# A layer with paged attention on one core: order of stores and gathers, values alone, and who scales and who adds

## The reference, cut to what matters

```python
x = x + einsum('bct,bcd->bdt', x, W0[cond])                  # mix of the 32 tokens, by a condition
x = x + x @ W.T + lora(x, A[adapter], Bm[adapter]) * s       # dense layer plus an adapter of rank 16
# attention: 8 query heads, 4 key heads, head size 32, window 128, blocks of 16 rows of a paged cache
q, k, v = x @ Wq.T, x @ Wk.T, x @ Wv.T;  q, k = rope(rms(q)), rope(rms(k))
k_blocks = k_blocks.at[blk, :, off, :].set(k)                # new rows are written into the cache first,
v_blocks = v_blocks.at[blk, :, off, :].set(v)                # and any sequence may read a block that another wrote
x = x + softmax(mask(q @ k_all.T * SCALE)) @ v_all @ Wo.T
x = x + x @ W3[expert] + b3[expert]                          # one of 16 experts for each sequence
```

## Time and profile before

| | us |
|---|---|
| median of three runs | 156.03 (155.38 to 156.3) |
| the profiled execution | 154.9 |
| its span in the trace | 153.1 |

### The profile page before, as it was taken

One profiled execution on the slowest core, in us unless ns is written; L12 is line 12 of the kernel. 1 busy time (PEld: TensorE's weight loads), 2 busy tenths in 40 slices (PEclk: granted clock), 3 DMA queues, 4 the chain that ended last, 5 costly groups with the idle time before them and its releaser, 6 DMA issues.

```text
span 153.1 us, 4138 instructions
## 1 busy us (share of the span) xinstructions
PE 117.3 (77%) x1418; PEld 91.0 (59%) x1418; DVE 88.8 (58%) x315; ACT 85.8 (56%) x236; POOL 62.0 (41%) x65
## 2 busy tenths in 40 slices
PE   7569599999989586076598392892599999999762
PEld 7559458998374163074466272672387787776631
DVE  0597988857528824860344003610867999989361
ACT  3119634698743629256589721472438878888200
POOL 7666779000008764787233300330333444734000
PEclk9999999999999977659969758699569999999999
DMA  3982999999963444799739998999976676766110
GB/s 94 244 249 62 370 424 407 423 405 374 395 173 100 132 119 114 247 313 392 315 110 269 422 355 210 401 377 279 253 232 205 197 242 204 222 207 180 37 39 34
DMA packets 29100, 37.60 MB, mean 246 GB/s; under 512 B 9497, under 2 KB 26781, under 8 KB 27438
## 3 DMA queue, kind: packets, MB, share of 16 engines
q1 hardware_dynamic: 26136, 23.98, 50.0%
q0 software_dynamic: 2528, 12.82, 22.2%
q10 hardware_dynamic: 416, 0.56, 1.2%
HBM read 31.39 MB, written 10.04 MB: 271 GB/s over the span
## 4 chain that ended last, share of the span: by engine, by line
DMA 42%; PE 20%; SPq 17%; issue 9%; POOL 5%; DVE 3%; ACT 2%; POOLq 1%; DVEq 0%
DMA kv_rows<-blkp 15%; DMA wr_rows<-blkp 11%; PE bank L1117 5%; DMA blkp<-wr_rows,patch_i 4%; PE bank L1063 4%; POOL wr_rows L500 4%; DMA blkp<-in_L_cond_W 4%; PE bank L1075 3%; PE bank L1128 3%; SPq L386 3%; DMA mask_rows<-span_m 3%; DMA scal<-in_L_cond_scalings 3%; SPq L364 2%; SPq L365 2%; SPq L348 2%
## 5 line engine op out<-in xcount | busy, mean ns | idle before, releaser
L520 POOL TENSOR_TENSOR xin_m<-xin_m,ri 128x704 f32<-128x704 f32 x15 | 21.8, 1454 | 44.4 <-DVE ri L924 44.4
L674 ACT ACTIVATE xin_m<-kvn_m,nb 128x176 f32<-128x176 f32 x64 | 27.6, 443 | 9.2 <-DVE nb L911 9.2
L911 DVE CUSTOM_DVE_ANT_0 kvn_m<-bank,mask_m 128x176 f32<-128x176 f32 x64 | 18.0, 336 | 14.6 <-PE bank L1063 11.0
L951 DVE TENSOR_TENSOR blkp<-blkp,cst 128x512 f32<-128x512 f32 x16 | 15.6, 1015 | 17.6 <-DMA blkp<-in_L_cond_W 17.6
L1063 PE MATMUL bank<-kt_m,natQ 32*64 32x176 f32 x256 | 15.7, 366 | 10.0 <-DVE nb L911 9.1
L1063 PEld LDWEIGHTS bank<-kt_m,natQ 32*64 32x64 f32 x256 | 9.5, 150 | 14.2 <-issue 13.1
L500 POOL DMA_INDIRECT wr_rows<-kvn_m,row_i x8 | 8.8, 1104 | 21.3 <-DMA wr_rows<-blkp 19.1
L684 ACT COPY x_m<-bank 128x512 f32<-128x512 f32 x16 | 9.4, 590 | 13.0 <-PE bank L1075 12.8
L1043 PE MATMUL bank<-cst,blkp 121*128 121x121 f32 (+1 forms) x48 | 9.0, 352 | 7.8 <-DMA blkp<-wr_rows,patch_i 7.8
L1043 PEld LDWEIGHTS bank<-cst,blkp 121*128 121x128 f32 (+1 forms) x48 | 7.3, 190 | 10.0 <-DMA blkp<-wr_rows,patch_i 9.0
L674 ACT ACTIVATION_READ_ACCUMULATOR xin_m<-kvn_m,nb 128x1 f32 x64 | 12.8, 200 | 0.0
(11 more groups left out here) (194 smaller groups left out, 257.4 us busy)
## 6 DMA issues: line engine op xcount, KB each, us to landing
blkp<-in_L_cond_W SPq DMA_DIRECT2D x32, 256.0 KB, 3.5
kv_rows<-blkp SPq DMA_DIRECT2D x3, 2048.0 KB, 10.3
wr_rows<-blkp SPq DMA_DIRECT2D x1, 1536.0 KB, 16.5
mask_m<-mask_rows SPq DMA_DIRECT2D x32, 44.0 KB, 5.4
vm_m<-kv_rows SPq DMA_DIRECT2D x4, 320.0 KB, 4.4
xin_m<-in_x SPq DMA_DIRECT2D x2, 512.0 KB, 5.6
out<-wq_m SPq DMA_DIRECT2D x8, 128.0 KB, 3.5
vm_m<-kv_rows SPq DMA_DIRECT2D x2, 384.0 KB, 4.6
```

The costliest lines, as they stand in the source:

```text
L520: pool.tensor_tensor(e_, e_, ri[:, p % 2, :].unsqueeze(2).broadcast_to([P, 4, KEYS]), ALU.mult).then_inc(s_pn, 1)
L674: act.activation(pr_seq(n % 2, u, j), S[:, n % 2, u, j, :], ACT.Exp, bias=nb[:, n % 2, 2 * u + j:2 * u + j + 1], scale=-1.0, accum_out=rs[ ...
L911: dve.tensor_tensor_reduce(S[:, n % 2, u, j, :], bank[2 + (2 * n + u) % 3][:, j * KEYS:(j + 1) * KEYS], mask[:, 2 * n + j, :], -SCALE, 3e3 ...
L951: tt(w_, w_, ident.unsqueeze(1).broadcast_to([P, B4, P]), ALU.add).then_inc(s_wx, 1)
```

## The change

- The store of the written blocks goes ahead of all masks, in SyncE's list; the masks come in smaller lots: 16 behind it, 4 behind `values_out(0)`, 4 behind `values_out(1)`, 8 behind `values_out(2)`. Each lot of 8 has its own semaphore, and VectorE waits for a lot at every fourth pair.
- GpSimd issues the gathers of units 1 and 2 only when both halves of NU are permuted. Their four permutes are all done by VectorE, behind the rotations; before, ScalarE did three of them.
- `values_out` stores the values alone (512 B pieces, 121 or 110 partitions) to `v_rows`, instead of keys and values of 128 partitions.
- Patches 0 and 1 are issued together, patch 2 behind the landing of `values_out(0)`.
- `values_out(u + 1)` stands behind four experts, no longer ahead of them. Experts 8 to 15 go to `blkp[1]`, not `blkp[2]`.
- Key chunks 4 and 5 are turned within the loop (two in each of the first four steps), and q tiles 4 to 7 in steps 3, 4, 6, 7. VectorE does the last six pieces of q's norm and rotation within the loop, one a step in steps 0 to 5.
- In the loop VectorE scales the probabilities of every pair, and GpSimd adds the identity to the expert weights and then gathers that group's bias.

```diff
-            for b in range(8):
-                load_mask(b)
             for kv in range(2):
                 sp.wait_ge(s_perm[NU, kv], 1)
             sp.dma_start(wr_blocks, blkw[0:NWI, :]).then_inc(s_base, 16)
-            for b in range(8, B):
+            for b in range(2 * MB):
                 load_mask(b)
...
-                        u = (0, 2)[b // 8]
+                        u = b // 8
                         sp.wait_ge(s_kt, 4 * (u + 1))
                         sp.wait_ge(s_vo[u], 16)
...
-                sp.dma_start(kv_rows[u], blkp[u][:, :]).then_inc(s_vo[u], 16)
+                sp.dma_start(v_rows[u, 0:PU[u]], by_o[u][0:PU[u], :, 1, :]).then_inc(s_vo[u], 16)
...
             values_out(0)
+            for b in range(2 * MB, 2 * MB + 4):
+                load_mask(b)
             values_back(0)
-            values_out(1)
             for b in range(4):
                 expert(b)
+            values_out(1)
+            for b in range(2 * MB + 4, 3 * MB):
+                load_mask(b)
             values_back(1)
-            values_out(2)
             for b in range(4, 8):
                 expert(b)
+            values_out(2)
+            for b in range(3 * MB, B):
+                load_mask(b)
             values_back(2)
...
-            for i in ((NU, 0), (NU, 1), (0, 0), (0, 1), (1, 0), (1, 1)):
+            for i in ((NU, 0), (NU, 1), (0, 0), (0, 1)):
                 load_blocks(i)
...
+            for kv in range(2):
+                pool.wait_ge(s_perm[NU, kv], 1)
+            load_blocks((1, 0))
+            load_blocks((1, 1))
             pool.wait_ge(s_l0, 4)
             load_blocks((2, 0))
             pool.wait_ge(s_vz, 1)
             load_blocks((2, 1))
...
-            for u in range(NU):
+            def patch(u):
...
+            patch(0)
+            patch(1)
+            pool.wait_ge(s_vo[0], 16)
+            patch(2)
             pool.wait_ge(s_eidi, 1)
             pool.wait_ge(s_l1, 4)
-            for n in range(NT):
-                pool.indirect_dma_start(out=be[n], ...)
-            for p in range(PAIRS - 1):
-                pool.wait_ge(s_ri, p + 1)
-                pool.tensor_tensor(e_, e_, ri..., ALU.mult).then_inc(s_pn, 1)
+            for g in range(NT):
+                pool.wait_ge(s_we[g % B4], 16 * B4 * (g // B4 + 1))
+                for kc in range(KC):
+                    w_ = We4(g)[:, :, kc, kc * P:(kc + 1) * P]
+                    ptt(w_, w_, ident.unsqueeze(1).broadcast_to([P, B4, P]), ALU.add).then_inc(s_wx, 1)
+                pool.indirect_dma_start(out=be[g], ...)
...
-            permute((2, 0))
+            for i in ((1, 0), (1, 1), (2, 0), (2, 1)):
+                permute(i)
...
                     dve.reciprocal(ri[:, p % 2, :], rs[:, p % 2, :]).then_inc(s_ri, 1)
+                    dve.wait_ge(s_ri, n)
+                    tt(e_, e_, ri[:, p % 2, :]..., ALU.mult).then_inc(s_pn, 1)
...
-                g = group_at(n, ADD_X)
-                ...
+                if n in Q_STEP:
+                    i, piece = Q_STEP[n]
+                    q_part[i][piece]()
```

More of the change, by code:

```diff
@@ L47 @@
 NE = 16
+MB = 8
 LAST = WINDOW + BLOCK - 2
@@ L296, in program @@
         s_wx = sem("residual_added")
-        s_be = [sem(f"expert_bias_loaded{i}") for i in range(2)]
+        s_be = [sem(f"expert_bias_loaded{i}") for i in range(NT)]
         s_out = [sem(f"output_written{i}") for i in range(2)]
@@ L632, in _ @@
             root_k(1)
-            permute((1, 0))
             keep_v(1)
@@ L659, in _ @@
                 keep_kt(c)
-                if c == 3:
-                    for t in range(2):
-                        keep_qt(t, bank[QT_BANK[0]][:, t * D:t * D + D])
-            for t in range(2):
-                keep_qt(2 + t, bank[QT_BANK[1]][:, t * D:t * D + D])
+            for t in range(4):
+                keep_qt(t, bank[QT_BANK[t // 2]][:, t % 2 * D:t % 2 * D + D])
+            root_q(2)
+            root_q(3)
+            act.activation(warm[:, 1:2], eps[:, 0:1], ACT.Exp)
             for n in range(PAIRS + TURN):
@@ L894, in _ @@
             rotations(0)
-            permute((2, 0))
+            for i in ((1, 0), (1, 1), (2, 0), (2, 1)):
+                permute(i)
             dve.wait_ge(s_rt, 8)
-            for i in range(4):
+            for i in range(2):
                 for piece in q_part[i]:
                     piece()
+            for i in range(2, 4):
+                q_part[i][0]()
             for n in range(PAIRS + RESULT):
@@ L944, in _ @@
                        bank[0][:, 0:D].rearrange("p (b c) -> p b c", b=B4)).then_inc(s_ot, 1)
-                g = group_at(n, ADD_X)
-                if g is not None:
-                    dve.wait_ge(s_we[g % B4], 16 * B4 * (g // B4 + 1))
-                    for kc in range(KC):
-                        w_ = We4(g)[:, :, kc, kc * P:(kc + 1) * P]
-                        tt(w_, w_, ident.unsqueeze(1).broadcast_to([P, B4, P]), ALU.add).then_inc(s_wx, 1)
+                if n in Q_STEP:
+                    i, piece = Q_STEP[n]
+                    q_part[i][piece]()
         @block.tensor
@@ L1204, in _ @@
             pe.wait_ge(s_x2, 4)
-            for t in range(2):
-                turn_q(t, bank[QT_BANK[0]][:, t * D:t * D + D])
-            for c in range(4, 6):
-                turn_k(c)
-            for t in range(2):
-                turn_q(2 + t, bank[QT_BANK[1]][:, t * D:t * D + D])
+            for t in range(4):
+                turn_q(t, bank[QT_BANK[t // 2]][:, t % 2 * D:t % 2 * D + D])
             scores(0)
@@ L1214, in _ @@
                     scores(n + 1)
-                for c in KT_STEP.get(n, ()):
-                    turn_k(c)
+                if n in KT_STEP:
+                    turn_k(KT_STEP[n][0])
                 g = group_at(n, PROJECT)
@@ L1225, in _ @@
                     layer3(g)
+                if n in KT_STEP:
+                    turn_k(KT_STEP[n][1])
             pv(PAIRS - 2)
```

78 lines of the change are left out of this document (34 added, 44 removed).

## The result

The changed kernel takes 161.44 us (median, 160.7 to 161.8). Against the kernel before on the same chip that is a ratio of 1.035, 95% interval 1.027 to 1.042: slower, where 144.0 was forecast. The profiled execution took 160.7 us, its span is 158.9 us. Some executions of any kernel are disturbed and take up to some per cent longer: the medians and ratios here are of the others, but the profiled executions of a2, b3, b4 and c2 were disturbed ones, 2 to 4% longer than the fastest of their kernel.

The account below looks back on a forecast made before the run. Transfers were taken to bound the kernel until the last one lets TensorE start `layer3(2)`, then a constant 32.6 us tail. -12.5 + 1.5 restart + 0.5 contention - 0.4 tail = -10.9 from 154.9 gives 144.0 us; 8-in-10 range 134.5 to 149.5.

Parts of the forecast that it names:

- First store: Writers' store, with no masks ahead: issued at 25.46, landing near 33.5 instead of 44.96.
- Scatters: Scatters of written blocks: first from 34, last issued near 45.5, patch 0 landing near 55.9 instead of 65.8.
- TensorE's path to the loop: From q's projection and patch 0 to `scores(0)`: loop start near 66.2, a gain of 7.3 us.
- SyncE's sum: Issues and flights of values stores, reads back, masks and experts added up: experts 8 to 11 landed 105.9, `layer3(2)` 108.0.
- eight of them nearly hide behind a flight: Masks behind the third values store: eight take 8.4 us against a flight of 8.
- Narrow stores spread badly: Rival, chance 0.2: values stores from 121 and 110 partitions use 11 DMA engines, flights 9.1 to 10 us; 148 us.
- The restart: TensorE's slow first round behind the stall ahead of `layer3(2)`: 1.5 us added.
- The loop: Contention of VectorE's scalings with GpSimd's additions in the rounds behind `layer3(2)`: 0.5 us in all.
- Rounds over 7 us: Sign of being wrong: rounds exceed 7 us because VectorE is blocked; 6.1 to 6.5 us expected.
- The 0.4 us of the tail: Scaling of pair 14 in the tail comes 0.9 us sooner, TensorE busy until 139.8: 0.4 us gained.
- The range: Forecast's own range 139 to 148 us; 8-in-10 range 134.5 to 149.5 us.
- The faster rival: Rival, chance 0.2: TensorE binds, `layer3(2)` at 99 to 102 without cold restart, 135 us.

Follow-up runs that it names:

- a2: Changed kernel with the last eight masks behind experts 8 to 11; time is that of the changed kernel (traced run 164.9 us).
- b3: Kernel before with the writers' store ahead of all 32 masks, gathers not held; the time is that of before.
- b4: b3 with values alone stored from all 128 partitions; layer3(2) at 120.3 as before, one untraced run of 149.6 us.
- c2: c1 with values stored from 128 partitions, store u+1 ahead of the experts, and GpSimd scaling, VectorE adding as before; 5% faster than before.
- d3: c4 with the four held gathers issued with the first four; slower, 4.6 us of the 5.8 forecast reached the end.
- c1: Changed kernel with six masks ahead of the writers' store, 26 behind it, none later; 8.1 us less than the changed kernel.
- a1: Changed kernel with values stored from all 128 partitions instead of 121 or 110; 4.8 us less.
- e1: c1 with the values stored from all 128 partitions; 1.3 us gained for the store's width.
- c4: c2 with the new roles (VectorE scales, GpSimd adds); 147.5 us.
- d2: c4 with GpSimd adding for groups 0 to 3, then scaling pairs 10 to 14, VectorE doing the rest; 145.9 us, 0.937 of before.
- d1: c4 with whole rows stored (128 pieces of 16 KB) instead of values alone (2048 of 512 B); 2.6 us worse.
- b1: Kernel before with the new roles alone (VectorE scales, GpSimd adds, bias gathered one group at a time); 3 us slower.
- c3: c2 with four experts ahead of each later values store; 5.7 us slower than c2.
- e2: d2 with roles changed back sooner (group 3 for 4, pair 8 for 10); slower, runs between 151.15 and 153.85 us.

## Why the prediction was wrong

The forecast for `layer3(2)` was 108.0, it was 120.1; the rest was to be 34.2 us (32.6 with restart, contention and tail), it was 38.8. 12.1 + 4.6 = 16.7 us, the whole error. By its steps:

- **First store: right.** Issued 26.4 (25.5), landed in 7.5 us (33.9; forecast 33.5). d3 shows the mechanism: without the held gathers the first scatter starts at 45.5 again.
- **Scatters: forecast 3.6 to 3.9 us too early.** The first went at 37.6, not 34, behind the first keys on VectorE; the last at 49.4, not 45.5. Patch 0 landed at 59.7 (55.9). The stretch was bound by two things, and I shortened one.
- **TensorE's path to the loop: right.** `scores(0)` at 67.3 (66.2).
- **SyncE's sum: the step that failed.** It was 3.9 us late at store 0. From there to store 2 it took 35.0 us and not 31.4. The flights were 9.3 and 9.9 us for 9.5 and 8.2, and the reads back with what stands before the experts 3.3 us each for 2.1. From store 2 to the reads back it took 12.6 us and not 8.8, since eight masks took 10.08 us and started 2.4 us behind the store: a mask costs 1.26 to 1.8 us beside 512 B pieces, not 1.03. From the reads back to `layer3(2)` it was 12.8 us and not 11.9. I priced the mask from its quiet row, while the other row of the same group gave 30.97 / 24 = 1.29. That eight of them nearly hide behind a flight was the sentence that decided, and it rested on the cheaper row. c1 prices the placement: 8.1 us in all, with `layer3(2)` 6.1 us sooner, 4.8 of them between the third store and its read back.
- **"Narrow stores spread badly" (0.2): it was so.** The store from 121 partitions moved 0.695 of the packets that the one from 128 moved in the same time. The Trainium skill's rule gives 11 of 16 engines for it (DMA: Bandwidth & Descriptors, Why a DMA increments its semaphore by 16 and not by 1), and the traces agree. I forecast 4 us for it, a1 gave 4.8 on the changed kernel, e1 1.3 once the masks were gone. I had it as a rival beside the forecast, though it needed nothing else to fail: it should have been in the sum.
- **The restart: right.** It was forecast at 1.5 us. The first round took 8.60 us and the next 7.13, and TensorE's clock was 0.50 in the first.
- **The loop: the second step that failed, 0.5 us forecast, 4.5 measured.** The rest of the span is 38.8 us for 32.8, and 1.5 of these 6.0 are the restart. I asked whether VectorE has room for the scaling (5.5 of 6.14 us), and it has. I did not ask what it stands ahead of. The scaling on GpSimd ran beside VectorE's copy; in VectorE's own list the copy waits 0.9 us for it, in each round, on TensorE's chain. d3 shows this part alone: at the full clock its rounds are 7.12, 7.13 and 7.10 us, and its rest is 35.7, 2.9 more than with the old roles. The 1.6 us that are left fall in the rounds of 7.99 and 7.55 us (7.10 and 6.91 in d3), where scalings took 1.79 and 1.58 us for 0.89 beside GpSimd's additions. That is the blocking that I priced at 0.5; no run takes it out alone. Rounds over 7 us were my own sign of it, but two thirds of the loop's loss were the place. The 0.4 us of the tail did not come: behind layer 3 of group 5 the times are 6.91 and 3.67 us in d3, 6.85 and 3.68 before.
- **The range** held neither. The faster rival (TensorE binds, 135) got as much chance as the narrow store; nothing ran below 144.8.

The change's idea is sound. With the masks in SyncE's first wait, stores from all partitions and store u+1 ahead of the experts, its order gives 147.5 us (c4), and with GpSimd scaling in the tail 145.9 (d2). That this is near the 144.0 of the forecast doesn't bear the forecast out: those kernels have a different list.

## What to carry to other kernels

When an order is moved forward, list what ran for nothing in the waits that the move leaves empty: here eight cheap instructions sat in such a wait, and with the masks put among the later transfers the kernel lost 8.1 us. Without that it is 2% faster than before (c1). Price an instruction on a busy queue from its row in traffic, not from its quiet one. And an operation moved to an engine with room must also be placed: ask which instruction of the critical chain now stands behind it.

## What the hardware showed beside that

- Issue on SyncE was slower behind a store of many pieces: the experts behind 2048 pieces took 10.9 us where 128 pieces left 6.9 (c4, d1). The first mask behind the changed kernel's first values store, at 62.23, stands with 2.98 us in its chain of waits.
- Engines stood without anything to wait for that the profile shows. ScalarE stood for some 5 us at 18 to 23 us in b1 to b4 and for 4 us up to 18.6 in the changed kernel, but not in before, c1, c3 or any d, with the same instructions up to there. Its timeline in b3:

```profile
23.09 2.05 ACT L549 COPY x_m<-bank 128x512 f32<-128x512 f32 x4 [5.00 <-remote]
```

In the changed kernel it cost little: c1 has no such wait, and its first scatter goes at 37.06 against 37.57. In b3 and b4 it held the writers' store and the masks by 3 to 4 us. The DMA engines were full then (0.99 in b3), but just as full in before (1.02), where ScalarE did not stand, and 85% busy in e2's gaps (108 to 116 us). What held these engines stays open.
